# GpSimd applies gamma and beta of two LayerNorm tiles in one operation instead of one tile at a time

## The reference

```python
h = relu(layernorm(x))                        # no gamma, beta
for l in range(3):                            # L0
    attn = softmax(where(mask, leaky(si + sj + b), -inf))
    h1 = layernorm(h + attn @ h, g1[l], beta1[l])
    ff = gelu(h1 @ W1[l] + b1[l]) @ W2[l] + b2[l]
    h  = layernorm(h1 + ff, g2[l], beta2[l])
x = x + h
x = x + elu(gat(relu(layernorm(x)), adj))     # L1
```

## Time and profile before

| | |
|---|---|
| median of 3 runs | 2385.7 us (2384.79 to 2389.38) |
| the profiled execution, its own time | 2381.08 us |
| its span in the trace | 2379.3 us |
| mean granted TensorE clock | 0.991 |
| busy: TensorE, weight loads, VectorE | 94%, 71%, 79% |
| busy: ScalarE, GpSimd | 66%, 48% |

### The profile page before, as it was taken

One profiled execution on the slowest core, in us unless ns is written; L12 is line 12 of the kernel. 1 busy time (PEld: TensorE's weight loads), 2 busy tenths in 40 slices (PEclk: granted clock), 3 DMA queues, 4 the chain that ended last, 5 costly groups with the idle time before them and its releaser, 6 DMA issues.

```text
span 2379.3 us, 41322 instructions
## 1 busy us (share of the span) xinstructions
PE 2234.9 (94%) x14575; PEld 1695.6 (71%) x14575; DVE 1891.4 (79%) x5049; ACT 1574.4 (66%) x2454; POOL 1142.0 (48%) x2124
## 2 busy tenths in 40 slices
PE   5989999998999999999999999999998999999988
PEld 4566676776767777777777778677776777667677
DVE  7877679767788888888888888888877877767785
ACT  5657566666576776676767676767756666666765
POOL 6434246464174553554555443645544444334643
PEclk9999999999999999999999999999999999999999
DMA  6311112011130112210211102301131010011000
GB/s 221 125 45 57 42 47 97 5 59 47 52 115 2 45 52 88 75 36 11 97 59 60 45 24 75 111 6 45 50 103 63 1 45 10 6 41 27 19 24 30
DMA packets 68309, 128.56 MB, mean 54 GB/s; under 512 B 15069, under 2 KB 55297, under 8 KB 65030
## 3 DMA queue, kind: packets, MB, share of 16 engines
q1 hardware_dynamic: 68102, 125.92, 15.7%
HBM read 111.21 MB, written 14.69 MB: 53 GB/s over the span
## 4 chain that ended last, share of the span: by engine, by line
PE 60%; DVE 21%; ACT 8%; POOL 5%; issue 4%; DMA 1%; POOLq 0%; SPq 0%; DVEq 0%; ACTq 0%
PE OB L1741 40%; PE FBB L1741 12%; PE RB L1741 4%; DVE pw L1329 4%; DVE mj L1305 3%; DVE gT L1343 3%; ACT nms L960 3%; PE TH L1741 2%; DVE st L1196 2%; ACT pw L943 2%; DVE junk L1247 1%; ACT FBB L932 1%; PE TH L1788 1%; POOL rs L685 1%; DVE nm L1354 1%
## 5 line engine op out<-in xcount | busy, mean ns | idle before, releaser
L1741 PE MATMUL OB<-xx,pw 128*128 128x257 f32 x4096 | 943.9, 385 | 11.0 <-DVE xc L1223 8.1
L1741 PEld LDWEIGHTS OB<-xx,pw 128*128 128x128 f32 x4096 | 765.4, 191 | 136.2 <-DVE xc L1223 13.9
L1741 PE MATMUL FBB<-hT,wb 128*128 128x512 f16 x2304 | 560.0, 381 | 16.6 <-DVE gT L1343 15.6
L1741 PE MATMUL OB<-wb,gT 128*128 128x256 f16 x4608 | 567.4, 274 | 5.2 <-DVE gT L1343 5.0
L1741 PEld LDWEIGHTS OB<-wb,gT 128*128 128x128 f16 x4608 | 450.5, 98 | 133.7 <-DVE gT L1343 8.6
L680 POOL TENSOR_SCALAR ve<-mv 128x2 f32<-128x2 f32 x256 | 60.6, 237 | 946.6 <-DVE mv L1199 938.4
L932 ACT ACTIVATE FBB<-FBB,wc 128x512 f32<-128x512 f32 x384 | 252.1, 656 | 246.7 <-PE FBB L1741 246.3
L1343 DVE TENSOR_TENSOR gT<-FBB,gT 128x512 f16<-128x512 f32 x384 | 262.7, 684 | 191.5 <-ACT gT L937 190.2
L1741 PEld LDWEIGHTS FBB<-hT,wb 128*128 128x128 f16 x2304 | 214.3, 98 | 225.9 <-DVE gT L1343 24.2
L943 ACT ACTIVATE pw<-pw,sj 128x512 f32<-128x512 f32 x512 | 334.7, 711 | 58.9 <-DVE pw L1329 58.4
L707 POOL TENSOR_TENSOR xc<-xc,gb 128x256 f32<-128x256 f32 x384 | 292.8, 762 | 44.0 <-ACT xc L907 42.8
(11 more groups left out here) (148 smaller groups left out, 2375.1 us busy)
## 6 DMA issues: line engine op xcount, KB each, us to landing
wb<-w_scratch SPq DMA_DIRECT2D x19, 2048.0 KB, 7.8
adjst<-in_adj SPq DMA_DIRECT2D x56, 512.0 KB, 3.8
xx<-in_x SPq DMA_DIRECT2D x16, 512.0 KB, 5.6
nm<-in_L_gnn_W SPq DMA_DIRECT2D x6, 1024.0 KB, 8.1
gb<-in_L_gnn_g SPq DMA_DIRECT2D x48, 128.0 KB, 2.7
adjst<-in_x SPq DMA_DIRECT2D x6, 1024.0 KB, 10.8
out_x<-adjst SPq DMA_DIRECT2D x48, 128.0 KB, 1.7
pw<-in_adj SPq DMA_DIRECT2D x4, 1024.0 KB, 10.2
```

The source lines that it names most:

```text
L1741: return pe.matmul(o, lhsT, rhs, start=first, stop=last)
```

## The change

`affine(kind, k, t)` becomes `affine_pair(kind, k, j)`, which treats tiles 2j and 2j + 1 with one multiply and one add on 512 columns. Gamma and beta, 256 columns each, are broadcast over the pair by a step of zero. Each operation raises its semaphore by 2 once both tiles are done, and the pair waits for both tiles at its start. The places where affine operations stand in GpSimd's program stay, and no other engine's program changes.

```diff
-            def affine(kind, k, t):
+            def affine_pair(kind, k, j):
+                t = 2 * j
                 gb, s = ((gb1, gb1_ready), (gb2, gb2_ready))[kind]
-                v = xc[:, k % 2, t, :]
-                o = (v, xx[:, slot(k), t, 0:D])[kind]
-                n = 8 * fi(k) + t + 1
+                v = xc[:, k % 2, t:t + 2, :]
+                o = (v, xx[:, slot(k), t:t + 2, 0:D])[kind]
+                n = 8 * fi(k) + t + 2
+                gamma, beta = (gb[:, r, :].unsqueeze(1).broadcast_to([P, 2, D]) for r in range(2))
...
-                pool.tensor_tensor(out=v, in0=v, in1=gb[:, 0, :], op=ALU.mult).then_inc(mul_done[kind], 1)
+                pool.tensor_tensor(out=v, in0=v, in1=gamma, op=ALU.mult).then_inc(mul_done[kind], 2)
                 pool.wait_ge(mul_done[kind], n)
-                pool.tensor_tensor(out=o, in0=v, in1=gb[:, 1, :], op=ALU.add).then_inc(aff_done[kind], 1)
+                pool.tensor_tensor(out=o, in0=v, in1=beta, op=ALU.add).then_inc(aff_done[kind], 2)
...
-                for t in range(HT, NT):
-                    affine(LN2, k, t)
+                affine_pair(LN2, k, 2)
+                affine_pair(LN2, k, 3)
```

More of the change, by code:

```diff
@@ L783, in ffn_step @@
                         j = (1, 3, 9, 11).index(n)
-                        affine(LN1, k, 2 * j)
-                        affine(LN1, k, 2 * j + 1)
+                        affine_pair(LN1, k, j)
                     if n == 1:
@@ L800, in ffn_step @@
                     if n == 13:
-                        affine(LN2, k, 0)
-                        affine(LN2, k, 1)
+                        affine_pair(LN2, k, 0)
                     if n == (9 if k in GAT_FFN_LATE else 5) and k in SUM_AT:
                         node_sum(SUM_AT[k])
-                affine(LN2, k, 2)
-                affine(LN2, k, 3)
+                affine_pair(LN2, k, 1)
                 if gat == 6:
@@ L818, in gat_step @@
                         x1_add(gat, t)
-                    affine(LN2, k - 1, 4)
-                    affine(LN2, k - 1, 5)
+                    affine_pair(LN2, k - 1, 2)
                     final(g, 0)
-                    affine(LN2, k - 1, 6)
-                    affine(LN2, k - 1, 7)
+                    affine_pair(LN2, k - 1, 3)
                     ln_rstd(LNG, gat, 0)
```

## The result

The changed kernel takes 2403.86 us in the median (2401.23 to 2405.66, 4 runs), the one before 2385.98 us: a ratio of 1.0072, 95% interval 1.0054 to 1.0089. By the ratio that is 17 us slower, where 8 were forecast. The profiled execution took 2403.54 us, with a span of 2401.8 us.

The account below looks back on a forecast made before the run. The prediction took TensorE (busy 94%) to set the pace. Terms of -3.8, +6.5, +5.4 and 0 made +8.1 us on 2385.7: 2394 us (+0.34%), range 2381 to 2408, the forecast's own 2391 to 2400.

Parts of the forecast that it names:

- rival 3: More than the sum: some of 154 off-chain holds reach the chain, 2407 us, or the broadcast costs, 2405 us; 14%.
- Unit cost: A GpSimd affine operation on 512 f32 columns takes 1.26 us, bounds 1.16 and 1.45 us.
- GpSimd's busy time: At 0.42 us less a pair, 96 pairs make GpSimd some 40 us less busy, nearly all off the chain.
- Gain on GpSimd's passages: Chain passes through affine pairs at ten places; nine gain 0.42 us each, one loses it waiting for its second tile: -3.8 us.
- The first tile comes later: A pair's first tile is handed on 1.1 to 1.5 us later, but its readers come at least 3.54 us after: 0.
- The four places: Column operations in steps 9, 13, 17 and 21, held by longer GpSimd operations, end 1.6 us later each: +6.5 us.
- The 14 scattered column operations: Held column operations elsewhere on the chain each pay 0.53 us more, 14% of them escape: +5.4 us.
- Off the chain: 154 held VectorE operations off the chain also get some 0.5 us each, 80 us in all; not in the sum.
- Score products: Fifteen held score products on the chain: twice the hold, half as often, so 0; bounds +8 and -6 us.
- The cancelling: Half of the 14 scattered column operations escape, giving 0.3 instead of 5.4 us: 2389 us, within 2381 to 2390.5; 24%.
- the faster one: With half as many GpSimd operations the holds on the chain thin out; at a third, -9.0 us, 2377 us; 14%.

Follow-up runs that it names:

- run 1: Changed kernel with each pair's place and start wait kept, but operations on 256 columns again (multiply, multiply, wait, add, add): 2390.7 us, ratio 1.0027 to the kernel before.
- Run 9: Changed kernel, with GpSimd waiting for VectorE's column operations before the first norm's first pair in steps 1, 2, 25, 26 and 27 only: 2395.4 us, 1.0042.
- run 12: Changed kernel with only the first norm's first pairs in steps 1, 2, 25, 26 and 27 narrow again: 2397.8 us, 1.0049.
- run 3: Changed kernel with only the second norm's pairs 512 columns wide, the first norm tile by tile as before: 2389.1 us, 1.0019.
- run 2: Changed kernel with only the first norm's pairs 512 columns wide, the second norm tile by tile as before: 2396.2 us, 1.0057.
- run 6: Kernel before, with GpSimd waiting in 16 steps for VectorE's column operations before the first norm's first pair: 2392.5 us, 1.0026.

## Why the prediction was right or wrong

The direction and the mechanism held; the size was half. The measured 2403.9 us lie within the stated 2381 to 2408, but above the forecast's own 2391 to 2400, in the part that rival 3 had added. Two terms of the sum were wrong in opposite ways, one too large and one too small, so that even the 8 us are partly luck.

*Unit cost.* 1.26 us forecast, 1.27 measured in the median of L709 and L711. The broadcast costs nothing that can be seen. The pair takes 2.66 us (1116.81 to 1119.47, below) and not 2.56, as the add starts 0.14 and not 0.08 us behind the multiply.

*GpSimd's busy time.* It fell by 75 us, not by some 40. The prediction counted 96 pairs, which is one norm's; with 192 the same 0.42 us give 80. No term of the sum rests on it. The "13% less GpSimd work" is the share of the affine work alone; of all of GpSimd's work it is 7%.

*Gain on GpSimd's passages, -3.8 us.* Not seen. The chain now passes through whole affine pairs at two places only (522.49 and 2269.88 us). I read that as VectorE having become later than GpSimd at the others, so that a faster GpSimd saves nothing there. No run isolates it.

*The first tile comes later, 0.* Right as far as it goes: no row of waits names a score product or a second residual behind an affine add. But run 1 is 6 us slower with narrow operations. I had priced the wait for the second tile at 0.37 us in four places. That it and the order of the operations together cost more is shown; 2.4 us of it are the double holds above, the rest isn't placed.

*The four places, +6.5 us.* This term was too large. Step 13 in the changed kernel, VectorE and then GpSimd, to set beside the earlier trace rows:

```profile
1117.01 1.10 DVE L1311 TENSOR_SCALAR ef<-M 128x4 f32<-128x4 f32 x1
1118.02 0.15 DVE L1312 TENSOR_TENSOR um<-s,M 128x4 f32<-128x4 f32 x1
1118.20 0.16 DVE L1314 SCALAR_TENSOR_TENSOR um<-um 128x4 f32<-128x4 f32 x1
1118.40 1.12 DVE L1317 TENSOR_TENSOR cc<-s,um 128x4 f32<-128x4 f32 x1
```

```profile
1116.81 1.27 POOL L709 TENSOR_TENSOR xc<-xc,gb 128x512 f32<-128x512 f32 x1
1118.22 1.28 POOL L711 TENSOR_TENSOR xc<-xc,gb 128x512 f32<-128x512 f32 x1
```

The first hold came out as worked out (1.10 us). Then the add started at 1118.22 instead of 0.08 us after the multiply, and L1314, at 1118.20, slipped in ahead of it. Two long holds in place of three short ones: 2.51 us from start to end against 2.04, so +0.5 us and not 1.6. Steps 9, 17 and 21 show the same, and four times that is 1.9 us.

*The 14 scattered column operations, +5.4 us.* Too small, and this is the step that failed. I let each hold grow by 0.53 us and their number, if anything, shrink: 0.39 us for each of the 14. But where one of two dependent operations was held before and the next slipped through (step 1 above), both are held now, at 1.0 us each: +1.5 us a place. The column operations in steps 1, 2, 25, 26 and 27 had five of the 14 holds, forecast to grow by 1.9 us together, and grew by 6.5. Run 9 gives 7 us back in these five steps, run 12 5 to 6.

*Off the chain.* The sum left the 154 other holds out and rival 3 priced them. Some did come in: from 44 to 61 holds on the chain. In the steady stretch, at the start of step 10 (a GAT step) of the changed kernel, where the same three took 1.34 us and were not on the chain:

```profile
885.56 1.15 DVE L1312 TENSOR_TENSOR um<-s,M 128x4 f32<-128x4 f32 x1
886.74 0.16 DVE L1314 SCALAR_TENSOR_TENSOR um<-um 128x4 f32<-128x4 f32 x1
886.93 1.18 DVE L1317 TENSOR_TENSOR cc<-s,um 128x4 f32<-128x4 f32 x1
```

The four steps that come back took 278.9 us from one opening activation to the next (925.4 to 1204.3) and take 281.6 (939.0 to 1220.6). With a granted clock of 1.00 in both, these 2.7 us are not the clock's. The way to step 4's opening activation is 12 us longer, and there the clock takes part. Before, then changed:

```profile
72.10:424.40 352.30, 324.05 (x2076) 233.69 (x2075) 277.49 (x729) 225.40 (x341) 157.59 (x289) 0.99 0.19 65
72.50:436.20 363.70, 330.46 (x2076) 237.03 (x2075) 287.72 (x729) 225.49 (x342) 143.62 (x224) 0.97 0.20 63
```

TensorE took 6.4 us longer for the same 2076 matmuls at a granted clock of 0.97 instead of 0.99. The sum had no term for it: a longer wait of TensorE can be followed by a time at its lower clock. In the medians it weighs less than between these two traces (0.988 to 0.990 in the changed kernel's executions, 0.988 to 0.993 in those of the kernel before beside the experiments). 3.5 of the 12 us lie between those of steps 0 and 1, a stretch that differs by 3 us between runs whose program is the same up to there, so single stretches that early are not to be read closely.

*Score products, 0.* The second product's group grew by 20 us, the first's by 2, and by the norm it is the second that does it: 161.8 us with that one wide (run 3), 144.4 with the first (run 2), 145.0 before. Run 3 is 0.19% slower, 4.5 us, with its new waits included, so the term was small, and whether it is nothing isn't shown.

*Rivals.* The cancelling and the faster one failed: 147 of 198 holds stayed, not half. The third came nearest, by holds off the chain that came in; its other half, a broadcast that costs, did not happen. What stays open is how the rest of the 6 us of run 1 divides between the wait for both tiles and the order of the operations, whether it adds to the holds in the changed kernel, and how much of the 17 us goes with TensorE's clock.

## What to carry to other kernels

Fewer and longer operations on GpSimd save GpSimd's time, but lengthen every hold of a VectorE operation that meets one; in this kernel, where GpSimd is half idle and VectorE feeds the engine that bounds, that was a bad trade. Price it by looking for tiny VectorE operations that take several times their median, above all chains of dependent ones, and count how many of a chain are held, not only how long. Letting GpSimd wait until such a chain is through paid only where nothing urgent stood behind it in GpSimd's program. And look at the granted clock of a stretch before you put all of its extra time down to a wait.

## What the runs showed of the hardware

A hold is sharp: for the column operations of both kernels it ends 0.14 us before the end of the GpSimd operation, whether that takes 0.73 or 1.27 us. A step of zero in an operand of GpSimd cost nothing measurable (1.27 us against 1.26 from the line through other widths). An operation of 128 columns has a mean of 477 ns, so cutting in half costs 0.2 us of GpSimd's time a cut. Between two dependent GpSimd operations lie 0.14 us, and a VectorE operation can slip in there: whether it does was decided in step 13 by 0.02 us. And a wait of TensorE of 2.6 us was followed by 3.4 us at a granted clock of 0.50 in step 8 of run 6, and by none in step 12 of the same run.
